# A chain of neural network blocks: decay products in row bands 64 apart, late B.C products moved behind the early ones

## What is computed

```
A = -exp(A_log) * dt                     # (b, L, 16 heads), dt = softplus(...)
B = (x @ W_B.T).reshape(b, L, 16, 64);  C = (x @ W_C.T).reshape(b, L, 16, 64)
X = x_in.reshape(b, L, 16, 8) * dt[..., None]
Lmat   = exp(segsum(A))                  # decay between two tokens, 0 above the diagonal
Y_diag = einsum('bclhn,bcshn,bhcls,bcshp->bclhp', C, B, Lmat, X)
# ... plus what earlier chunks carry over; the sum equals, over the whole sequence:
# y[l] = sum over s <= l of (C[l].B[s]) * exp(cumsum(A)[l] - cumsum(A)[s]) * X[s]
out = (Y * silu(z)) @ W_out.T
```

## Time and profile before

| | |
|---|---|
| median of 3 runs | 717.67 us |
| the profiled execution's own time | 716.94 us |
| its span, first to last instruction | 715.0 us |
| busy: PE, DVE, ACT, POOL | 673.6, 570.6, 417.0, 323.9 us |
| Mamba steps (32) | 430.8 to about 597 us of the span |
| first decay of sections 0 to 7 | 430.83, 453.08, 475.05, 496.52, 517.18, 538.05, 558.99, 579.88 us |

### The profile page before, as it was taken

How to read it: one execution, slowest core, us unless ns; L and a number is a source line. 1 busy time by engine, 2 the same in 40 slices (tenths; PEclk the granted TensorE clock), 3 DMA queues, 4 the chain that set the end, 5 groups by cost and what they waited for, 6 DMA issues and landing times. The chain is left out here.

```text
span 715.0 us, 12393 instructions
## 1 busy us (share of the span) xinstructions
PE 673.6 (94%) x4100; PEld 501.8 (70%) x4100; DVE 570.6 (80%) x1311; ACT 417.0 (58%) x756; POOL 323.9 (45%) x404
## 2 busy tenths in 40 slices
PE   7899998697899999999999988999999998999997
PEld 5677774543457777777778776777777775777786
DVE  5899978889978888987989867676766676879775
ACT  4657676885246555556656666555565654455554
POOL 2668873101227766456757543220413200555463
PEclk9999999999999999999999999999999999999999
DMA  6635520000013233222313100000000000323131
GB/s 175 199 102 179 162 86 1 0 1 1 1 49 129 68 113 90 80 69 76 104 54 93 34 1 1 2 3 1 1 2 0 0 2 1 119 75 119 54 125 45
DMA packets 34345, 43.16 MB, mean 60 GB/s; under 512 B 5232, under 2 KB 17520, under 8 KB 34288
## 3 DMA queue, kind: packets, MB, share of 16 engines
q1 hardware_dynamic: 34288, 42.46, 19.6%
HBM read 41.13 MB, written 1.31 MB: 59 GB/s over the span
## 5 line engine op out<-in xcount | busy, mean ns | idle before, releaser
L728 POOL TENSOR_TENSOR p_prod<-p_p,p_gate_row 128x512 f32<-128x512 f32 x128 | 203.6, 1602 | 106.6 <-DVE p_p L524 62.5
L399 ACT ACTIVATE p_sil<-p_ps_a 128x512 f32<-128x512 f32 x176 | 105.1, 597 | 131.8 <-PE p_ps_a L100 127.5
L529 DVE TENSOR_TENSOR p_hlo<-p_prod,p_hhi 128x512 fp32r<-128x512 f32 x176 | 150.0, 854 | 0.3 <-ACT p_hhi L408 0.2
L524 DVE TENSOR_TENSOR p_p<-p_sil,p_ps_b 128x512 f32<-128x512 f32 x128 | 87.2, 681 | 51.9 <-ACT p_sil L399 37.3
L408 ACT CAST p_hhi<-p_prod 128x512 fp32r<-128x512 f32 x176 | 107.9, 615 | 22.4 <-POOL p_prod L728 22.3
L98 PE MATMUL p_ps_a<-xt_hi,w_uphi 128*128 128x512 f32 x176 | 74.2, 422 | 0.0
L98 PE MATMUL p_ps_acc<-p_hhi,w_downhi 128*128 128x512 f32 x176 | 71.1, 404 | 1.2 <-DVE p_hlo L529 1.0
L98 PE MATMUL p_ps_b<-xt_hi,w_uphi 128*128 128x512 f32 x176 | 71.0, 404 | 0.1
L100 PE MATMUL p_ps_a<-xt_hi,w_uplo 128*128 128x512 f32 x176 | 70.1, 398 | 0.0
L99 PE MATMUL p_ps_a<-xt_lo,w_uphi 128*128 128x512 f32 x176 | 70.1, 398 | 0.0
L100 PE MATMUL p_ps_b<-xt_hi,w_uplo 128*128 128x512 f32 x176 | 69.8, 397 | 0.0
(11 more groups left out here) (363 smaller groups left out, 1421.7 us busy)
## 6 DMA issues: line engine op xcount, KB each, us to landing
p_gate_row<-gate_rows SPq DMA_DIRECT2D x128, 256.0 KB, 3.3
w_rawbuf<-in_L_ffn_fc_w_dram SPq DMA_DIRECT2D x3, 512.0 KB, 5.9
w_rawbuf<-in_L_ffn_w_dram SPq DMA_DIRECT2D x3, 512.0 KB, 5.9
w_rawbuf<-in_L_ffn_shared_w_dram SPq DMA_DIRECT2D x3, 256.0 KB, 3.8
out_dram<-x SPq DMA_DIRECT2D x3, 256.0 KB, 3.6
x<-in_L_attn_x_dram SPq DMA_DIRECT2D x2, 256.0 KB, 3.8
x<-in_L_attn_x_dram SPq DMA_DIRECT2D x1, 512.0 KB, 8.3
mb_xraw<-in_L_attn_W_B_dram SPq DMA_DIRECT2D x1, 512.0 KB, 4.9
```

The source lines that it names most:

```text
L399: nc.scalar.activation(sil[:, u % 2], ps_a[:, u % 2], ACT.Silu).then_inc(c["sil"].sem, 1)
L524: nc.vector.tensor_tensor(dst, sil[:, u % 2], ps_b[:, u % 2], ALU.mult).then_inc(c["p1"].sem, 1)
L529: nc.vector.tensor_tensor(hlo[:, u % R], prod[:, u % R], hhi[:, u % R].bitcast(F32), ALU.subtract).then_inc(c["hlo"].sem, 1)
L728: G.tensor_tensor(prod[:, u % R], p1[:, u % 2], gate_row[:, e % ROWS], ALU.mult).then_inc(c["prod"].sem, 1)
```

## The change

Two edits in TensorE's program of the Mamba phase.

The first gives the late half another group of heads than the early half in the same step: `group_of(q, 1)` is q ^ 2. So the two decay matmuls of a step read the bands 0 and 64, 32 and 96, 64 and 0, 96 and 32 (first row of each). Products and outputs of the late half follow with their heads; over four steps every head still comes once for each half.

The second moves the late products of a step from behind the outputs to directly behind the early products.

```
+        def group_of(q, t):
+            return q ^ 2 if t else q
...
             def decay(h, m, q):
-                band = slice(32 * q, 32 * q + 32)
                 for t in range(2):
+                    band = slice(32 * group_of(q, t), 32 * group_of(q, t) + 32)
...
             def products(h, m, q, t, more):
-                    hd = head_of(q, k)
+                    hd = head_of(group_of(q, t), k)
...
             def outputs(h, m, q):
-                        hd = head_of(q, k)
+                        hd = head_of(group_of(q, part == 1), k)
...
             def section(...):
                     decay(h, m, q)
                     products(h, m, q, 0, more)
+                    products(h, m, q, 1, more)
                     if q == 3 and not more:
                         tail.turn_y(pe, m - 1, ps_y)
                     ...
                         outputs(...)
-                    products(h, m, q, 1, more)
```

## The result

The changed kernel takes 714.98 us, median of ten runs (711.94 to 716.65), where the kernel before took 718.5 in ten runs beside them (716.87 to 719.94). The ratio is 0.9949, 95% interval 0.9933 to 0.9964: some 3.7 us faster. Forecast were 4.7 us less and a time of 713.0; the median of the kernel before had itself come out 0.8 above the 717.67 from which the forecast started. One run of all those in this document is left out of its time and ratio, a fourth one of the last experiment, which took 929.83 us at a granted clock of 0.655.

A forecast was written before the change was run, and what follows sets the result against it. TensorE's program and a chain over VectorE and ScalarE both bound plain steps at 4.85 us. Terms 1.6 + 0.5 + 0.1 + 0.7 + 0.2 + 1.0 + 0.6 = 4.7 us took 717.67 to 713.0, range 709.8 to 717.0.

The forecast's parts named there:

- What bounds the kernel: In a plain step TensorE's program and the chain decay, cap, exp, copy, multiply, piece, next decay both take 4.85 us.
- The decays: A step's two decays, in different bands, overlap: 0.22 us saved, products 0.44 behind the first in place of 0.66.
- rival D: Paired decays stream at half pace, so cap and chain-bound steps grow by 0.22 us: 1.1 slower, 718.8; chance 0.07.
- The order: Late products beside early ones save one of five changes of shape a step: 0.20 us in all 32 steps.
- The new wait: On TensorE, late products wait for ScalarE's copy of the piece before; it ends 0.3 us early enough, costing 0.
- What the late products give to others: Late products start 1.1 us earlier, so VectorE's q 3 cap comes in time: 0.5 us over sections 3 to 6.
- The sum: Over the Mamba steps, TensorE's saving of 0.42 us each, with the chain's 3.23 us as floor, gives 4.7 us.
- The clock: Where Mamba joins the next block, the 1.2 GHz stretch moves but keeps its idling: 0, with 1.3 us either way.
- The numbers: For the whole kernel: forecast's chance 0.60, own range 711 to 715; chance of faster, below 714.1, 0.61.
- A: A step's two decays don't overlap; only the saved change of shape counts: 3.2 us, time 714.5; chance 0.13.
- B: TensorE alone bounds the steps and the chain shortens with it: 13.4 us, time 704.3; chance 0.05.
- C: VectorE and ScalarE are late also in q 0, q 3, sections 0 to 2: 2.2 us, 715.5; chance 0.15.

The follow-up runs named there:

- the last experiment: Split copy and multiply with one edit each, against the kernel before: new bands 712.48 us, ratio 0.9901; new order 711.15 us (median of three), 0.988.
- the shorter chain: Changed kernel with ScalarE's copy and VectorE's early multiply each made in two halves, piece starting after the first bank: 707.4 us, ratio 0.9854 to the kernel before.
- the split on the kernel before: Kernel before, without either edit, with ScalarE's copy and VectorE's early multiply each made in two halves: 715.07 us, ratio 0.9961.

## Why the prediction was right, and where its sum was off

**What bounds the kernel.** Right. The plain step kept its 4.85 us with 0.42 idle, and it took the shorter chain to lower it (4.47 us). Adding 0.44 us to TensorE cost nothing in it.

**The decays.** Right: 0.01 us apart, products 0.43 behind the first (0.44 forecast), 0.22 to 0.23 us a step by the bands alone. The cap starts 0.62 us behind the first decay as before, so rival D's delay is zero. By that number the semaphore tail of the Trainium skill ("TensorE: Matmul & The Clock Gate", Part 3, the per-tile semaphore tail) does not fall on the first of the pair here.

**The order.** Right in size: the new order takes 0.19 to 0.21 us off TensorE's step, the forecast 0.20. That this is the price of one change of shape is argued, not shown; no run changes the shape and nothing else. The drain that the Trainium skill names ("TensorEngine Tiling (Array Packing)", Tiling Modes, key properties) would be in it; no run separates it from the weight load behind it, so the split into 0.10 and 0.10 stays open.

**The new wait.** Free in q 1 to q 3, as forecast: all sixteen products run through. The early products of q 0 were under-priced. Section 4, the answer to the earlier trace rows:

```profile
516.40 1.01 ACT L2088 COPY mb_bc<-mb_c 128x1024 f32<-128x1024 f32 x1 [1.39 <-PE mb_c L100]
...
516.92 0.50 PE L1926 MATMUL mb_d<-w_downhi 32*128 32x512 f32 x1
516.92 0.49 PE L1926 MATMUL mb_d<-w_downlo,w_downhi 32*128 32x512 f32 x1
517.55 0.70 PE L1951 MATMUL mb_c<-mb_bc 64*128 64x256 f32 x4
...
520.27 0.38 PE L98 MATMUL mb_c<-xt_hi,w_uphi 128*128 x1
```

The copy ends at 517.41, and the products start 0.14 later, 0.63 behind the decay where I had taken 0.56. The piece comes 3.35 behind the decay in place of 3.25. With the bands alone this step gets only 0.03 us shorter, with the order alone 0.21, with both 0.19: in q 0 the overlap of the decays is worth next to nothing, since ScalarE's copy ends behind it. In q 0 of sections 2 and 7, outside the hardware loop, they start 0.56 and 0.55 behind the decay, as taken.

**What the late products give to others.** Right for q 3: VectorE's cap comes 0.62 us behind the decay where it came 0.72 behind it. The bands alone bring that too, since they also start the late products earlier.

**The sum**, term by term, forecast and then measured in the starts of the decays:

| term | forecast | measured |
|---|---|---|
| q 1, sections 3 to 6 | 1.6 | 1.70 |
| q 3, sections 3 to 6 | 0.5 | 0.42 |
| q 2 and q 3, sections 1 and 2 | 0.1 | 0.33 |
| q 0, sections 4 and 6 | 0.7 | 0.39 |
| q 0, sections 3 and 5 | 0.2 | 0 |
| section 0 q 3, section 1 q 0, section 2 q 0 | 1.0 | 0.94 |
| section 7 | 0.6 | 0.33 |
| together | 4.7 | 4.1 |

The mis-sized term is q 0, by 0.5; section 7 gave 0.3 less than forecast and sections 1 and 2 gave 0.2 more, so that the total comes nearer than its parts, partly by luck. For q 0: in section 5 the chain holds it (the cap comes 0.89 us behind the decay before and after), in section 3 the multiply, at whose end (3.19 us behind the decay) the piece came 0.16 later, before and after. Section 7 went as forecast on VectorE, the answer to the earlier trace rows:

```profile
583.31 1.28 DVE L2230 TENSOR_TENSOR mb_sm<-mb_sm,mb_c 128x512 f32<-128x512 f32 x2 [0.67 <-ACT mb_off L2110]
```

Every pair now takes 1.28 us (1.48 at one place before) and the idle 0.39 is gone: 0.76 us less between the first caps of q 0 and q 3. About half of that went again with the granted clock, the answer to the earlier trace rows:

```profile
593.20:600.00 6.80, 5.97 (x38) 3.79 (x29) 0.74 (x3) 3.13 (x5) 0.00 (x0) 0.50 0.00 0
```

The 1.2 GHz level begins at 593.2, behind idle time of TensorE in section 7's last step, and covers the last outputs of the phase (0.67 us for eight matmuls that took 0.40 in other steps).

**The clock.** I had counted 0, since the change "leaves its idling". In the profiles this did not hold, though it stayed within the 1.3 us allowed: the level lasted 3.4 us before (597.2 to 600.6) and 6.8 after (593.2 to 600.0), and TensorE's idle time ahead of the last output projection grew from 1.01 to 1.66 us. It cost about 0.43 us inside the phase, and the 0.55 behind it appears while the level lasts. Whether the change moves this stretch or the run does is not shown: the profiles of the bands alone and of the split on the kernel before have none here, those of the bands 32 apart and of both edits with the split have 6.8 us of it, and each is one execution.

**The numbers.** The time of 714.98 lies at the upper end of the forecast's own range, 711 to 715, and not below 714.1, where I had put 0.61 of the chance. Two sums are slightly off: 713.0 less 1.3, 1.2 and 0.5 is 710.0, not 709.8, and 0.48, 0.09 and 0.05 make 0.62, not 0.61.

**Rivals.** A is excluded by the decays' starts, B by q 2 at 4.85 us, D by the cap at 0.62. C is right only for q 0 of sections 3 and 5, which did not give: of the 2.5 us that it denies 2.1 came.

## What to carry to other kernels

When TensorE shows no idle time in a step, follow the piece of work that ends the step back over the other engines before pricing a saving: here two bounds lay on top of each other, so that an estimated 13.4 us saved on TensorE (32 steps of 0.42) brought 4.1. A cheap way to tell them apart is to add work to one engine and see in which steps it costs nothing. Once the other chain holds the step, cut a link of it in pieces that free a buffer sooner, and leave the order on all engines alone: moving a link ahead failed twice, on a copy that it had been hiding and on buffers that were not yet free.

## What the runs showed of the hardware

- Two 32-row matmuls in different bands of the array, writing different banks, start within 0.01 us of each other, 32 rows apart as well as 64. The first takes 0.49 to 0.50 us as before; the second shows 0.50 beside it and 0.39 behind it in one band, 0.34 us later. The matmuls that follow start 0.43 us behind the first, 0.66 with both in one band.
- The order with one change of matmul shape less (64-row products beside products instead of behind the outputs) is 0.19 to 0.21 us shorter on TensorE.
- In this kernel's sections 3 to 6, inside the hardware loop, the first products of q 0 start 0.14 us behind the end of the copy that releases them, outside it 0.05 to 0.06.
- A multiply of half the columns takes 0.42 us where the whole takes 0.69, but two of them in a row take 0.75: 0.06 more. Two half copies take 0.63 in place of 0.57.
- The granted clock dips in other places from run to run: 0.57 and 0.79 in the same 8 us near the start, of the changed kernel and the one before. Between these two profiles the work ahead of the change differs by 1.55 us, partly with it, which is why steps were compared and not only totals.
